# Pairing the exps of an attention loop: one activation over two score banks

## The reference

```python
q = (x @ Wq + bq).reshape(Bsz, Tlen, 8, 128)      # 8 query heads
kv = x @ Wkv + bkv                                # one key and one value head
q = transpose(q, (0, 2, 1, 3)) + pe;  k = kv[..., :128] + pe;  v = kv[..., 128:]
scores = einsum('bhqd,bkd->bhqk', q, k) / sqrt(128)
scores = where(causal, scores, finfo.min)
probs = softmax(scores, axis=-1)
attn = einsum('bhqk,bkd->bhqd', probs, v)
x = layernorm(x + attn_reshaped @ Wo)
...
x = layernorm(x + ffn(x))
```

## Time and profile before

| | |
|---|---|
| time, median of 3 runs | 4872.04 us (4856.91 to 4882.17) |
| profiled execution, its own time | 4852.79 us |
| span of its slowest core | 4851.2 us (cores 4808.0 to 4851.2) |
| mean granted TensorE clock | 0.67 of full speed on every core |
| PE (TensorE matmul) busy | 2595.9 us, 54% |
| ACT (ScalarE) busy | 1839.3 us, 38% |
| DVE (VectorE) busy | 1485.0 us, 31% |
| exps L374 | 1280, 848.0 us busy |
| PV matmuls L398 | 5120, 635.7 us busy |
| score matmuls L366 | 1280, 598.1 us busy |

### The profile page before, as it was taken

How to read it: one execution, slowest core, us unless ns; L and a number is a source line. 1 busy time by engine, 2 the same in 40 slices (tenths; PEclk the granted TensorE clock), 3 DMA queues, 4 the chain that set the end, 5 groups by cost and what they waited for, 6 DMA issues and landing times.

```text
span 4851.2 us, 64777 instructions; the slowest of 8 cores (4808.0 to 4851.2 us)
## 1 busy us (share of the span) xinstructions
PE 2595.9 (54%) x19792; PEld 1465.7 (30%) x19792; DVE 1485.0 (31%) x3689; ACT 1839.3 (38%) x3808; POOL 18.2 (0%) x35
## 2 busy tenths in 40 slices
PE   4766745332376664544356666464336666645441
PEld 1333424211133342432123334242113333334210
DVE  1322144222332213433323221443233222144332
ACT  0355633210325564331034556433122555533213
POOL 0000000000000000000000000000000000000000
PEclk9778866555677786555576788665558678756555
DMA  4200052468410001026731000104852000010564
GB/s 89 61 18 18 1 113 71 85 125 168 113 40 23 11 8 61 36 65 147 129 99 44 18 18 1 61 36 87 171 107 100 18 18 18 22 57 19 135 135 130
DMA packets 174812, 324.86 MB, mean 67 GB/s; under 512 B 5654, under 2 KB 136982, under 8 KB 168986
## 3 DMA queue, kind: packets, MB, share of 16 engines
q10 hardware_dynamic: 140224, 117.45, 11.8%
q1 hardware_dynamic: 26330, 163.94, 11.4%
q0 software_dynamic: 7936, 39.33, 4.8%
HBM read 239.95 MB, written 120.07 MB: 74 GB/s over the span
## 4 chain that ended last, share of the span: by engine, by line
PE 43%; DMA 18%; ACT 17%; issue 11%; DVE 10%; ACTq 1%; SPq 1%; DVEq 0%; POOL 0%; POOLq 0%
PE pp_s L366 8%; PE pp_pv L398 8%; DMA rpe<-rp_scratch 8%; DMA rp_scratch<-rpn 8%; PE pp_w L477 5%; ACT pT L374 5%; PE pp_s L303 5%; PE pp_s L679 4%; PE pp_s L648 3%; PE pp_s L731 2%; ACT x2b L637 2%; ACT pTn L420 2%; PE pp_pv L731 2%; DVE x L485 2%; DVE st_m L817 1%
## 5 line engine op out<-in xcount | busy, mean ns | idle before, releaser
L374 ACT ACTIVATE pT<-pp_s,c_negC 128x512 bf16<-128x512 f32 x1280 | 848.0, 691 | 324.1 <-PE pp_pv L398 315.0
L398 PE MATMUL pp_pv<-vS,pT 128*128 128x129 bf16 x5120 | 635.7, 261 | 140.4 <-DVE pT L382 133.7
L366 PE MATMUL pp_s<-qT,kT 128*128 128x512 bf16 x1280 | 598.1, 485 | 182.7 <-ACT pT L374 145.0
L398 PEld LDWEIGHTS pp_pv<-vS,pT 128*128 128x128 bf16 x5120 | 451.4, 115 | 385.9 <-issue 360.5
L382 DVE TENSOR_TENSOR pT<-pT,c_zl 128x512 bf16<-128x512 bf16 x512 | 217.6, 425 | 931.9 <-ACT pT L374 930.7
L731 PE MATMUL pp_s<-w_2t,inr 32*64 32x256 bf16 x1024 | 143.3, 401 | 595.9 <-DVE rpn L744 502.0
L303 PE MATMUL pp_s<-xT,w_q 128*128 128x512 bf16 x1024 | 230.6, 389 | 282.5 <-DMA w_kv<-cwkv 213.3
L744 ACT CAST rpn<-pp_s 128x256 bf16<-128x256 f32 x256 | 95.4, 372 | 726.1 <-DMA rpe<-rp_scratch 654.5
L477 PE MATMUL pp_w<-w_o,atT 128*128 128x512 bf16 x1024 | 261.6, 414 | 93.8 <-DVE x L485 79.8
L744 DVE CAST rpn<-pp_s 128x256 bf16<-128x256 f32 x256 | 108.7, 424 | 612.5 <-DMA rpe<-rp_scratch 561.0
L731 PEld LDWEIGHTS pp_s<-w_2t,inr 32*64 32x64 bf16 x1024 | 72.7, 122 | 661.8 <-issue 658.8
(11 more groups left out here) (86 smaller groups left out, 2813.7 us busy)
## 6 DMA issues: line engine op xcount, KB each, us to landing
rp_scratch<-rpn SPq DMA_DIRECT2D x32, 2048.0 KB, 17.9
rpe<-rp_scratch ACTq DMA_DIRECT2D x32, 2048.0 KB, 23.9
xtile<-x SPq DMA_DIRECT2D x64, 512.0 KB, 3.8
y<-x SPq DMA_DIRECT2D x64, 512.0 KB, 4.5
w<-cw ACTq DMA_DIRECT2D x12, 2048.0 KB, 7.9
w_2t<-cw ACTq DMA_DIRECT2D x48, 512.0 KB, 11.9
xT<-xT POOLq DMA_DIRECT2D x4, 4096.0 KB, 25.7
w<-w POOLq DMA_DIRECT2D x4, 2048.0 KB, 16.1
```

The source lines that it names most:

```text
L366: return inc("tensor", "sPE", 1, lambda e, kc=kc, ping=ping, h=h, qb=qb: e.matmul(pp_s[ping][:, :], kT[:, kc * 128: kc * 128 + 128], qT[:, ...
L374: ev = inc("scalar", "sACT", 1, lambda e, ping=ping: e.activation(out=pT[ping][:, :], in_=pp_s[ping][:, :], func=AF.Exp, bias=c_negC, scal ...
L398: ping=ping, sub=sub, kc=kc, kcmax=kcmax: e.matmul(bank[:, colo: colo + 129], pT[ping][:, sub * 128: sub * 128 + 128], vS[:, kc * 132: kc ...
```

## The change

The two score banks become one PSUM tensor `pp_sp` of 128 x 1024 in float32 with `pp_s[0]` and `pp_s[1]` as its halves, and the two `pT` buffers one tensor `pTp` with halves. `emit_exp` becomes `emit_exp_pair`: one activation reads both banks and writes both halves. It is emitted once for two chunks, behind both of their score matmuls, and it waits for the guards of both halves of `pT`. Its mark stands for both chunks. The loop over chunks goes in steps of two: scores(kc + 2), scores(kc + 3), PV(kc), PV(kc + 1), then the exp of the pair kc + 2, kc + 3. The masks stay one for each chunk. The squares write to the same places as before.

```diff
-    pT = [at(f"pT{i}", [128, 512], BF16, r4 + T * 2 + NT * 132 * 2 + i * 1024)
-          for i in range(2)]
+    pTp = at("pTp", [128, 1024], BF16, r4 + T * 2 + NT * 132 * 2)
+    pT = [pTp[:, 0:512], pTp[:, 512:1024]]
...
-    pp_s = [nc.alloc_psum_tensor(f"pp_s{i}", [128, 512], F32).ap() for i in range(2)]
+    pp_sp = nc.alloc_psum_tensor("pp_sp", [128, 1024], F32).ap()
+    pp_s = [pp_sp[:, 0:512], pp_sp[:, 512:1024]]
...
-            def emit_exp(h, kc, sv, exp_m, mask_m):
-                ping = kc % 2
+            def emit_exp_pair(h, kc, sv, exp_m, mask_m):
                 wait("scalar", sv)
-                gwait("scalar", ("pT", ping))
-                ev = inc("scalar", "sACT", 1, lambda e, ping=ping: e.activation(
-                    out=pT[ping][:, :], in_=pp_s[ping][:, :], func=AF.Exp,
+                gwait("scalar", ("pT", 0)); gwait("scalar", ("pT", 1))
+                ev = inc("scalar", "sACT", 1, lambda e: e.activation(
+                    out=pTp[:, :], in_=pp_sp[:, :], func=AF.Exp,
                     bias=c_negC, scale=cfg.SCALE))
-                exp_m[kc] = ev
-                gset(("ps", ping), ev)
-                j = kc - 4 * qb
-                if j >= 0:
-                    wait("vector", ev)
-                    mv = inc("vector", "sDVE", 1, lambda e, ping=ping, j=j: e.tensor_tensor(
-                        pT[ping][:, :], pT[ping][:, :],
-                        c_zl[:, (3 - j) * 128: (3 - j) * 128 + 512], ALU.mult))
-                    mask_m[kc] = mv
+                exp_m[kc] = ev; exp_m[kc + 1] = ev
+                gset(("ps", 0), ev); gset(("ps", 1), ev)
+                for k2 in (kc, kc + 1):
+                    j = k2 - 4 * qb
+                    if j >= 0:
+                        wait("vector", ev)
+                        mv = inc("vector", "sDVE", 1, lambda e, ping=k2 % 2, j=j: e.tensor_tensor(
+                            pT[ping][:, :], pT[ping][:, :],
+                            c_zl[:, (3 - j) * 128: (3 - j) * 128 + 512], ALU.mult))
+                        mask_m[k2] = mv
...
-                sv = emit_scores(h, 0, exp_m)
-                emit_exp(h, 0, sv, exp_m, mask_m)
-                if kcmax > 1:
-                    sv = emit_scores(h, 1, exp_m)
-                    emit_exp(h, 1, sv, exp_m, mask_m)
+                emit_scores(h, 0, exp_m)
+                sv = emit_scores(h, 1, exp_m)
+                emit_exp_pair(h, 0, sv, exp_m, mask_m)
                 if h > 0:
                     emit_epilogue_tensor(h - 1)
-                for kc in range(kcmax):
-                    nxt = kc + 2
+                for kc0 in range(0, kcmax, 2):
                     sv = None
-                    if nxt < kcmax:
-                        sv = emit_scores(h, nxt, exp_m)
-                    epi["pv_last"] = emit_pv(h, kc, kcmax, exp_m, mask_m)
+                    if kc0 + 2 < kcmax:
+                        emit_scores(h, kc0 + 2, exp_m)
+                        sv = emit_scores(h, kc0 + 3, exp_m)
+                    epi["pv_last"] = emit_pv(h, kc0, kcmax, exp_m, mask_m)
+                    epi["pv_last"] = emit_pv(h, kc0 + 1, kcmax, exp_m, mask_m)
                     if sv is not None:
-                        emit_exp(h, nxt, sv, exp_m, mask_m)
+                        emit_exp_pair(h, kc0 + 2, sv, exp_m, mask_m)
```

More of the change, by code:

```diff
@@ L258, in emit_ln2_finish @@
             inc("scalar", "sACT", 1, lambda e, tt=tt: e.activation(
-                out=pT[0][:, :], in_=x2[:, tt * 1024: tt * 1024 + 512],
+                out=pT[0], in_=x2[:, tt * 1024: tt * 1024 + 512],
                 func=AF.Square, accum_out=st_v[:, tt: tt + 1]))
             inc("scalar", "sACT", 1, lambda e, tt=tt: e.activation(
-                out=pT[1][:, :], in_=x2[:, tt * 1024 + 512: tt * 1024 + 1024],
+                out=pT[1], in_=x2[:, tt * 1024 + 512: tt * 1024 + 1024],
                 func=AF.Square, accum_out=st_r[:, tt: tt + 1]))
```

## The result

The changed kernel takes 5625.3 us (median of 10 runs, 5619.5 to 5638.4) against 4861.4 (median of 10 runs of the kernel before, 4851.9 to 4903.3): a ratio of 1.1559, interval 1.1531 to 1.1586. It is 15.6% slower. All medians, ratios and intervals here leave out executions in which one die ran at a lower clock than the other and the time was some per cent longer. The profiled execution has a span of 5618.0 us, 767 more than before.

The account below looks back on a forecast made before the run. It took the attention loop as ScalarE and TensorE taking turns, TensorE the bound at 1.2 GHz. Heads' 781 us plus 7 for block starts, 788, on the 4872 median gave 5660; it predicted 5650, range 5570 to 5760.

Parts of the forecast that it names:

- the sum: Loss over all attention heads at 1.2 GHz: 781 us, plus 7 us at the blocks' first exps, 788 us together.
- The waits: Attention loop: exp waits for the previous pair's PVs, next scores for the exp; no buffer left, overlap of ScalarE and TensorE gone.
- The sign given for TensorE: Expected in the profile after: TensorE's scores wait for the exp, 1.3 us a pair.
- first rival: Attention clock stays at 2.4 GHz, gaps of 1.11 + 0.35 us being too short to lower it: some 5190 us, chance 0.05.
- A pair: One pair of chunks within a head at 1.2 GHz takes 3.39 us, against 2.06 before.
- the two scores: Term of a pair's round trip at 1.2 GHz: two score matmuls, 2 x 0.43 = 0.86 us.
- the starts of the blocks: At each of 16 block starts the first exp waits for two scores in place of one: 16 x 0.43 = 7 us.
- The exp: ScalarE's merged exp of 1024 columns takes 1.11 us, bounds 1.05 and 1.27, where two separate exps take 1.27.
- The end of a head: Last pair of a head, with masks unhidden, to the next head's first exp: 1.11 + 1.71 + 1.70 = 4.52 us.
- The clock: TensorE at 1.2 GHz (granted 0.50) throughout attention, as in the first block before; chance 0.86.
- The rival of the high clock: Only long idle gaps lower TensorE's clock, so attention stays at 2.4 GHz: some 5190 us, chance 0.05.
- A gain: Rival: the merged exp saves ScalarE 0.16 us a pair, 640 times, 102 us, giving 4770 us; chance 0.02.

Follow-up runs that it names:

- two_pT: The changed kernel with a second pair of pT buffers and still one pair of score banks: 5128 us, ratio 1.052.
- two_psum: The changed kernel with a second pair of score banks (the output projection's) and still one pair of pT: 5143 us, ratio 1.056.
- two_both: The changed kernel with a second pair of score banks and a second pair of pT, exp still merged: 4628 us, ratio 0.953.
- tail_split: The changed kernel with only the last pair of each head as two separate exps, each with its mask behind it: 5589 us, ratio 1.148.
- filler: The changed kernel with idle matmuls added behind each pair of PVs and ahead of each head's transposes: 5193 us, ratio 1.067.
- order_only: The kernel before with the changed order (two scores, two groups of PVs, two separate exps), nothing merged: 5231 us, ratio 1.075.
- single_four: The changed kernel with four score banks and four pT, but two separate exps of 512 columns for the merged one: 4572 us, ratio 0.939.
- cross_single: The kernel before with four score banks, four pT and a block's heads as one stream, all exps separate: 4464 us, ratio 0.917.

## Why the prediction was right

The median of 5625 is 25 under the 5650 predicted and inside the range. The median before was 4861 in ten runs; with the 788 us of the sum that makes 5649, so the miss lies in the sum: 788 against 764. By its steps:

- **The waits.** Right, and the cause: one round trip, with each engine idle while the other works. It is shown from both sides by two_pT, two_psum and two_both: with one buffer more on either side part of the loss goes, with both all of it. The sign given for TensorE, 1.3 us a pair, was added up wrongly: the prediction's own terms make 1.46 (1.11 + 0.35, as in its first rival), and 1.46 was measured.
- **A pair.** 3.39 predicted, 3.34 measured. The term that was off is the two scores, 0.80 from the first start to the PVs in place of 0.86; the earlier trace rows have 0.38, not 0.43, from a score to the PVs behind it. The four heads together hold 16 such pairs, so 512 in all, 26 us. The heads as a whole are 18 us below the sum (71.76 against 72.32, times 32), so their first and last pairs took some 8 us more than forecast. The other 6 of the 24 are most of the 7 put down to the starts of the blocks.
- **The exp.** 1.11 predicted, 1116 ns measured. The estimate worked out from the Trainium skill, page "ScalarE: Activation LUTs", section "What ACT_TABLE_LOAD costs", was 1133 ns, 1.5% above the row.
- **The end of a head.** 4.52 predicted, and 4.52 measured in the changed kernel's first block (exp at 160.88, next at 165.40), the place of the earlier trace rows:

```profile
160.88 1.11 ACT L374 ACTIVATE pTp<-pp_sp,c_negC 128x1024 bf16<-128x1024 f32 x1 [2.23 <-PE pp_pv L399]
162.10 0.76 DVE L383 TENSOR_TENSOR pTp<-pTp,c_zl 128x512 bf16<-128x512 bf16 x2 [2.25 <-ACT pTp L374]
...
162.67 1.03 PE L399 MATMUL pp_pv<-vS,pTp 128*128 128x129 bf16 x8 [1.89 <-DVE pTp L383]
...
165.40 1.13 ACT L374 ACTIVATE pTp<-pp_sp,c_negC 128x1024 bf16<-128x1024 f32 x1
```

  That it is on the path, tail_split showed.
- **The clock.** 1.2 GHz in all blocks, as chosen. It was read off a stretch of the kernel before with about the same work in the same time. By filler the clock was worth 424 of the 763 us. The rival of the high clock was that of the Trainium skill, page "TensorE: Matmul & The Clock Gate", section "HAM oscillation — how this bites in real kernels", by its words on long gaps. The trace doesn't bear it out: the clock stayed at 0.50 although TensorE was never idle for more than 1.9 us at a time in the four stretches (1.46 in a pair, at most 1.89 at the end of a head). It shows a clock that doesn't rise; one that was up and falls can't be seen in it. filler, with the clock held up by added work, shows that the rival's sum was sound as a price: 5193 us, where I had 5190.
- **A gain.** The merge by itself never paid in what was measured: with the same order and buffers, separate exps were faster in order_only (5231 against 5625) and single_four (4572 against 4628), and not slower in cross_single. Its 134 us of ScalarE are real, but they came back as waiting.

## What to carry to other kernels

Merging two instructions of a double-buffered loop into one over both buffers halves the number of buffers in units of work: two banks of one chunk become one bank of one pair, and the loop turns into a round trip. Count the buffers in units of the new instruction before merging, and double them first; here the score banks came from an idle PSUM tensor and the room in SBUF from a later stage's. Then measure the same buffers without the merge: here they did as well or better, and the gain was theirs. And price a new wait on TensorE twice: once as idle time, and once as the clock of everything around it, by finding a stretch of the old trace where TensorE did about the same work in the same time.

## What the hardware showed that I had not expected

TensorE's clock was at 0.50 in the first block of the kernel before, and idle matmuls into unused banks brought the same block of the changed loop to 1.00; with 2784 such matmuls the kernel took 7.7% less time than without (5193 us against 5625). A second mask right behind the first costs VectorE less than I took: two take 0.76 us, not 2 x 0.42.
